# Two attention layers on one core: the values' products taken for four key blocks at a time, nine buffers of exponentials, new order tables

## The reference

```python
# layer 0, per image
h = group_norm(x, 32 groups) * gn_w + gn_b
q, k, v = split(qkv_w @ h + qkv_b)              # per head: 32 x 1024 each
w = softmax((q * s).T @ (k * s))                # 1024 x 1024, 8 heads
y = x + proj_w @ (v @ w.T) + proj_b
# layer 1, per image
q, k, v = Wq @ y, Wk @ y, Wv @ y                # 32, 32, 256 rows
out = gamma * (v @ softmax(q.T @ k).T) + y
```

## Time and profile before

| | |
|---|---|
| median of three runs | 1522.86 us |
| profiled execution, its own time | 1526.38 us |
| its span, first to last instruction | 1524.6 us |
| TensorE, matmuls: busy | 1483.1 us, 97% |
| GpSimd busy | 1185.9 us, 78% |
| VectorE busy | 1099.2 us, 72% |
| ScalarE busy | 746.4 us, 49% |
| mean granted TensorE clock | 0.977 of full |

### The profile page before, as it was taken

One profiled execution on the slowest core, in us unless ns is written; L12 is line 12 of the kernel. 1 busy time (PEld: TensorE's weight loads), 2 busy tenths in 40 slices (PEclk: granted clock), 3 DMA queues, 4 the chain that ended last, 5 costly groups with the idle time before them and its releaser, 6 DMA issues.

```text
span 1524.6 us, 20547 instructions
## 1 busy us (share of the span) xinstructions
PE 1483.1 (97%) x7216; PEld 891.4 (58%) x7216; DVE 1099.2 (72%) x1922; ACT 746.4 (49%) x1373; POOL 1185.9 (78%) x548
## 2 busy tenths in 40 slices
PE   8899999999999999999999999999999999999878
PEld 6444445577455855558555775558555684457447
DVE  4777878777787778877687777877788686765343
ACT  2256455544565354653555445653546435554411
POOL 2189988985989679995989859896799959898703
PEclk9699899999999999999999999999999999999979
DMA  5233031301403014120413014030231214000100
GB/s 140 55 96 68 17 87 46 83 10 49 112 22 84 15 56 102 39 65 28 112 50 79 12 51 111 22 84 15 60 100 41 60 31 109 22 1 8 49 21 28
DMA packets 47143, 85.24 MB, mean 56 GB/s; under 512 B 11072, under 2 KB 21184, under 8 KB 47040
## 3 DMA queue, kind: packets, MB, share of 16 engines
q1 hardware_dynamic: 46896, 83.74, 21.7%
q10 hardware_dynamic: 144, 0.20, 0.1%
HBM read 18.29 MB, written 8.39 MB: 17 GB/s over the span
## 4 chain that ended last, share of the span: by engine, by line
PE 87%; DVE 5%; SPq 3%; issue 2%; ACT 1%; DMA 1%; POOL 0%; ACTq 0%; DVEq 0%; POOLq 0%
PE work L635 15%; PE st L551 15%; PE pv L582 15%; PE pv L560 14%; PE work L698 7%; PE work L669 4%; DVE mpart L931 3%; PE work L705 3%; PE work L657 3%; SPq L386 3%; PE st L543 2%; PE work L643 2%; PE rec L599 2%; PE work L663 1%; PE rec L612 1%
## 5 line engine op out<-in xcount | busy, mean ns | idle before, releaser
L902 POOL TENSOR_TENSOR acc<-acc,probs 128x1024 f32<-128x1024 f32 x380 | 889.7, 2382 | 49.1 <-ACT probs L773 49.1
L773 ACT ACTIVATE probs<-st 128x512 f32<-128x512 f32 x1152 | 611.2, 601 | 446.1 <-PE st L551 326.7
L931 DVE TENSOR_REDUCE mpart<-work 128x1 f32<-128x512 f32 x1008 | 635.8, 680 | 164.8 <-PE work L635 163.2
L635 PE MATMUL work<-ks,qs 96*128 96x512 f32 x1008 | 427.0, 464 | 8.7 <-DMA ks<-part_hi 3.6
L551 PE MATMUL st<-qs,ks 98*128 98x512 f32 x1024 | 398.3, 436 | 6.2 <-DMA qs<-mrow 3.1
L902 POOL TENSOR_TENSOR acc<-probs 128x1024 f32<-128x1024 f32 x64 | 150.9, 2376 | 165.6 <-ACT probs L773 165.3
L635 PEld LDWEIGHTS work<-ks,qs 96*128 96x128 f32 x1008 | 191.7, 193 | 148.9 <-DVE mpart L931 87.9
L551 PEld LDWEIGHTS st<-qs,ks 98*128 98x128 f32 x1024 | 193.7, 191 | 126.1 <-ACT probs L773 67.8
L560 PE MATMUL pv<-probs,vt 128*32 128x512 f32 x2048 | 247.9, 602 | 0.0
L582 PE MATMUL pv<-probs,l_vt 128*128 128x256 f32 x1024 | 240.2, 383 | 0.5 <-ACT raw L839 0.5
L582 PEld LDWEIGHTS pv<-probs,l_vt 128*128 128x128 f32 x1024 | 193.2, 191 | 34.1 <-ACT probs L773 5.9
(11 more groups left out here) (82 smaller groups left out, 940.0 us busy)
## 6 DMA issues: line engine op xcount, KB each, us to landing
qs<-part_hi SPq DMA_DIRECT2D x120, 128.0 KB, 2.4
ks<-part_hi SPq DMA_DIRECT2D x120, 128.0 KB, 2.4
xa<-in_x SPq DMA_DIRECT2D x16, 512.0 KB, 4.3
y<-in_x SPq DMA_DIRECT2D x8, 1024.0 KB, 5.6
out<-raw SPq DMA_DIRECT2D x32, 256.0 KB, 2.2
qs<-part_lo SPq DMA_DIRECT2D x60, 128.0 KB, 2.4
ks<-part_lo SPq DMA_DIRECT2D x60, 128.0 KB, 2.4
l_qs<-part_hi SPq DMA_DIRECT2D x32, 64.0 KB, 2.0
```

The source lines that it names most:

```text
L635: last = mm(bank, qs[g][0:HI_HI_LO, c, j, tb * P:(tb + 1) * P], ks[g][0:HI_HI_LO, j, half * HALF:(half + 1) * HALF], start=True, stop=True)
L773: nc.scalar.activation(probs[:, n % PRING, half * HALF:(half + 1) * HALF], st[:, (2 * n + half) % ST_BANKS, :], ACT.Exp).then_inc(s_exp1 i ...
L902: pool.tensor_tensor(a, first, probs[:, n % PRING, :], ALU.add).then_inc(s_add0, 1)
L931: last = dve.reduce_max(mpart[:, 4 * j + tb, half:half + 1], bank, AX.X)
```

## The change

- `PRING` is 9 instead of 6. The memory comes from `raw1`, which is no longer a tile of its own: layer 1's results now lie in `xa`, and the low parts of `QF` in `y`. `mrow` is shared by the two groups of heads.
- Bursts stand at n % 8 == 1 and take four key blocks: 16 matmuls in the program, 32 in the trace. There are 64.
- The load of the next image into `xa` waits until the stores of the step before are done; the first load of `y` stands behind the stacking of `qs` and `ks` of the second group; `T` waits for the other group's rows.
- ScalarE, at slots with n % 8 == 1, serves the entries of the first two stops ahead of its exponentials.
- All four tables have new numbers. In the epilogue layer 1's first token half (`QK1`, `VT1` for n = 0) now stands ahead of the last `SUM`, and one `VT1` stands behind all maxima and their transposition.

```diff
-PRING = 6
+PRING = 9
...
 EPILOGUE = {
-    "sums": (2, 3, 3, 3, 3),
-    "layer1": (0, 0, 5, 6, 7, 9, 9, 10, 12, 13),
-    "maxima1": (11, 11, 11, 11, 15, 15, 15, 15, 15, 15, 15, 15, 15, 15, 15, 15, 16, 17),
+    "sums": (2, 10, 11, 11, 11),
+    "layer1": (0, 0, 0, 1, 6, 11, 11, 11, 17, 53),
+    "maxima1": (23, 33, 33, 33, 33, 33, 33, 33, 33, 33, 33, 33, 33, 33, 33, 33, 42, 42),
...
-        raw1 = sb("raw1", [P, 4, KT, QUARTER])
...
-        mrow = [[sb(f"mrow{g}{c}", [16, 2, P], F32R) for c in range(2)] for g in range(GROUPS)]
+        mrow = [sb(f"mrow0{c}", [16, 2, P], F32R) for c in range(2)]
...
+        def raw1(c):
+
+            return xa[:, c // 2, c % 2 * HALF:(c % 2 + 1) * HALF].rearrange("p (m t) -> p m t", m=KT)
...
                     sp.wait_ge(s_h, KT * (b + 1))
+                    if b > 0:
+                        for c in range(4):
+                            sp.wait_ge(s_out[c], 16 * b)
                     for k in range(KT):
                         sp.dma_start(xa[:, k, :], x_v[b + 1, :, k, :]).then_inc(s_x, 16)
...
                     if n == 1 and kind not in ("prologue", "first"):
-                        product_l0(SLOTS - 3, b - 1)
-                        product_l0(SLOTS - 1, b - 1)
-                    elif n % 4 == 1 and n - 5 in units and unit_use(n - 2)[0] == 0:
+                        for m in range(SLOTS - 7, SLOTS, 2):
+                            product_l0(m, b - 1)
+                    elif n % 8 == 1 and n - 9 in units and unit_use(n - 2)[0] == 0:
                         ci = unit_use(n - 2)[1] // 16
-                        if unit_use(n - 2)[1] % 16 == 3:
+                        if unit_use(n - 2)[1] % 16 == 7:
...
-                        product_l0(n - 4, b)
-                        product_l0(n - 2, b)
+                        for m in range(n - 8, n, 2):
+                            product_l0(m, b)
...
-                    entries = [e for k in range(STOPS) for e in plans[kind][STOPS * n + k]]
+                    stops = [plans[kind][STOPS * n + k] for k in range(STOPS)]
+                    before = stops[0] + stops[1] if n % 8 == 1 else []
+                    for e in before:
+                        use_entry(e, kind, b)
                     if n in units:
                         exponentials(n, kind, b)
```

More of the change, by code:

```diff
@@ L61 @@
+    "qk1": (193, 196, 196, 203),
+    "norm": (27, 34, 35, 42, 52, 70, 84, 100, 109, 110, 120),
+    "sums": (10, 14, 14, 16, 23, 72, 74, 75, 100, 118, 134, 135, 135, 141, 146, 153, 154, 154, 154, 157),
+    "sums1": (159, 159, 159, 162, 164, 164, 170, 171, 175, 175, 193, 193),
+    "v0": (181, 206),
+    "layer1": (4, 7, 32, 33, 38, 55, 88, 112, 139),
+    "v1": (14, 16),
+    "maxima": places(1, 0, 1, 2, 2, 2, 1, 0, 0, 1, 2, 2, 0, 0, 0, 3, 1, 1, 1, 1, 0, 0, 1, 0, 2, 0, 1, 0, 0, 0, 1,
[6 rows of a table added]
 }
 FIRST = {
-    "qf": (7, 7, 8, 8),
@@ L77 @@
+    "qk1": (158, 193, 208, 209),
+    "norm": (31, 31, 31, 42, 48, 53, 55, 104, 105, 107, 110),
+    "sums": (60, 72, 85, 87, 109, 118, 122, 151, 156, 158, 177, 179, 192, 203, 206),
+    "v0": (193, 212),
+    "v1": (32, 48),
+    "maxima": places(4, 0, 1, 0, 0, 1, 1, 0, 0, 0, 0, 3, 0, 2, 0, 0, 0, 0, 0, 0, 0, 0, 0, 2, 0, 0, 0, 2, 0, 1, 0,
[6 rows of a table added]
 }
 LAST = {
[L79 to L80 removed]
@@ L938, in use_bank @@
                         ahead = 1 if (g, c) == (0, 0) else 0
-                        rows, src, done, hi_done, n = (mrow[g][c], bank[0:16, 0:P], s_mrow[g][c], s_mhi[g][c], b + ahead)
-                        if kind not in ("prologue", "first") or (kind == "first" and ahead):
-                            dve.wait_ge(done, 32 * n)
+                        rows, src, hi_done, n = mrow[c], bank[0:16, 0:P], s_mhi[g][c], b + ahead
+                        if g:
+                            dve.wait_ge(s_mrow[0][c], 32 * (b + 1))
+                        elif n > 0:
+                            dve.wait_ge(s_mrow[1][c], 32 * n)
                     else:
```

70 lines of the change are left out of this document (30 added, 40 removed), and 36 rows, old and new, of tables (EPILOGUE, FIRST, LAST, STEADY).

## The result

The changed kernel takes 1516.56 us in the median of five runs (1513.55 to 1517.52), against 1522.86 (1521.46 to 1525.66, five runs) of the kernel before beside it: a ratio of 0.9947, with the interval 0.9936 to 0.9959, so 8.1 us less (the two medians themselves are 6.3 apart). Forecast were 23.3 less. The time lies at the upper edge of the range.

The account below looks back on a forecast made before the run. TensorE, busy 97%, was taken as the bound, with GpSimd 10.6 us behind in the long stretch. Terms -23.9 + 7 - 2 - 4.4 = -23.3 us gave a forecast of 1499.5 us, range 1485 to 1517.

Parts of the forecast that it names:

- (1): TensorE's bursts of products: 128 become 64, 63 of them count at 0.38 us each, 23.9 us less.
- (2): Waits behind longer bursts, with VectorE idle 1.8 us in each: 1.0 us a step, +7 in all, at worst +17.
- rival A: VectorE's idle time in each burst is paid by TensorE afterwards: 1511.6 us, chance 0.17.
- (3): Nine buffers of exponentials: needed for the long bursts, but little gain by themselves, 0 us.
- (4): Moved tiles, later loads, shared `mrow` and ScalarE's new order: 0 us; up to 1 us a step if the load's cover goes.
- (5): First step: less TensorE work before slot 10 brings first units and everything after earlier, -2 us, ends -6 and +3.
- (6): The end, from the last `SUM` to layer 1's scores: moved work fills idle time, -4.4 us, ends -7 and +1.
- D: The 0.4 us belong to each pair of key blocks, so merging bursts saves nothing: 1516 us, chance 0.07.
- C: GpSimd runs dry in bursts and sets a slower pace: 1525 us at 1 us a step, 1548 at 5; chance 0.08.

Follow-up runs that it names:

- both readers are light: Layer 0's maxima over half the keys and most exponentials over half the queries, in both kernels: 1488.17 us on the kernel before, 1462.89 on the changed kernel.
- the light GpSimd: GpSimd's additions from the second of a chunk on over half the elements, in both kernels: 1521.61 us on the kernel before, 1514.04 on the changed one.
- the new end alone: The kernel before with only the epilogue's new table: 1519.4 us, 0.996 of the kernel before.
- VectorE light: Layer 0's maxima reduced over 256 of 512 keys, in both kernels: 1497.16 us on the kernel before, 1486.57 on the changed kernel.

## Why the prediction was wrong

**(1) The bursts: right in price.** 0.375 us each against 0.38, from starts in one steady step, and 18.1 us for 48 bursts where both readers are light.

**(2) The waits behind a longer burst: right in kind, too small, and with only half of the cause.** I had 1.0 us a step; it is (18.0 - 9.4) / 6 = 1.4. I named VectorE, and ScalarE "likewise" had three exponentials, but I priced only VectorE's 89%. Measured, neither is the payer alone: either reader of the banks takes back about half of the bursts' price even when the other is light (a maximum 0.42 us instead of 0.68, an exponential 0.38 instead of 0.60). The Trainium skill, "TensorEngine Tiling (Array Packing)", section Performance Considerations, which I weighed under rival A, warns that tiling leaves the emptying of PSUM as it is; the trace agrees in that the two emptying engines together hold back half of the gain. Both kernels are tiled alike, so what tiling itself does to the emptying no run here shows.

**(3) Nine buffers, (4) the moved tiles: right for the steady steps**, 1066.6 against 1067.6 us. Not for the first step with its old table, where the missing slots 48 to 55 make slot 56 wait for the unit before it: 2.8 us and more, gone with ten buffers. In the changed kernel the tenth buffer brings nothing there.

**(5) The first step: the step that failed.** Predicted -3.7 with its seven bursts and the wait, measured +4.7: 8.4 of the 12.6 us by which the profiles miss the forecast. Its ground was that GpSimd works 79.5 of 80 us there, "so what brings the first units earlier moves everything after". The first units do come earlier, 1.5 us at slot 10, but nothing after moves with them: at slot 18 the step is 2.6 us behind, at its end 4.7. And the light GpSimd has 64 us less to do in the step and ends it no sooner (199.9 against 199.3). A full engine was taken for the bound. Instead, table and bursts each cost time by themselves. With the old table the long bursts add 3.4 to 4.2 us (205.3 against 202.0 and 201.1) though they save seven ways in and out; with short bursts the new table is 1.6 to 3.3 us dearer than the old one (203.6 and 204.4 against 202.0 and 201.1), the smaller figure within the scatter of 2.4. Together they are no dearer than either alone. Which wait of TensorE carries this stays open.

**(6) The end: right between its marks, and in part by luck.** From `SUM` to the scores it is 4.4 us less, as forecast. But the sum took what moved ahead of `SUM` for free. There the changed kernel is 2.0 us longer, though most of the last step's eight bursts (3.0 us) are saved in it; with the new end alone it is 4.0 longer. What was not in the sum, 3.6 us less from the scores to the end, where the granted clock is 0.97 instead of 0.89, makes up for most of that: -6.0 for the last step and the end instead of -7.4.

**The sum** was to be -23.3. By the stages it is +4.7 - 9.4 - 6.0 = -10.7, by the ratio of the runs -8.1. Rival A had 1511.6 us, "(2) is +17 or more, and (5) gives nothing": nearer in size than the forecast, but its mechanism, VectorE alone, is only half of what happens. (D's 1516 us lies nearest of all, by accident: its mechanism, a cost that is not the burst's, is excluded by the starts.) GpSimd as the bound, C, is excluded by the light GpSimd. The signs that I had named for the forecast mostly came: 3.57 us a burst, some 176 us from `P` to `P`, 31.7 us from `SUM` to the scores, no doubled wait of weight loads for VectorE. Only VectorE's own wait for the maxima fell where it was to grow. None of them looked at the first step or at the time ahead of `SUM`, so they could not tell that the sum would fail.

## What to carry to other kernels

Merging short runs of another shape saved a fixed price each time, here 0.375 us, and stretched the gap in which the other readers get nothing. Whether the saving stayed depended on both engines that empty TensorE's banks: lightened one at a time, the test said "not this one" for each of them. So lighten the suspects together as well before you let one go. Ask of work that is moved what it pushes back where it goes, and name a sign for each stage of the sum. A row of waits that appears (92.8 us) or a full engine (79.5 of 80 us) is a suspicion, and one more buffer or a halved operation settles it for a few runs.

## What the runs showed of the hardware

The order at the end bears on the clock of the last 40 us: with 3.27 us of idle time ahead of the scores the first sixteen products took 5.86 us and the stretch had a granted clock of 0.89; with `VT1` in that gap they took 3.62 us, at 0.97 to 1.00, in eleven of 13 profiles, and 4.8 us, at 0.92, in two.

The way into narrow matmuls cost 0.10 to 0.20 us in the bursts shown and the way out 0.13, whether 16 or 32 of them stood between. The Trainium skill, "TensorEngine Tiling (Array Packing)", section Tiling Modes, says that a change of the mode drains the engine; these rows show its price here. Not all of the way in is that: in the earlier trace rows the burst's first weights had waited for ScalarE's exponentials, as the timeline of the weight loads shows, and with VectorE light the mean way in is 0.12 us instead of 0.16.

```profile
786.69 0.16 PEld L560 LDWEIGHTS pv<-probs,vt 128*32 128x32 f32 x8 [0.24 <-ACT probs L773]
```

In the first step a single burst of 32 can fall into a spell of the lower level; on the timeline of after it is 5.27 us instead of 3.64:

```profile
83.77 5.27 PE L567 MATMUL pv<-probs,vt 128*32 128x512 f32 x32
```

and the window of it has a granted clock of 0.65:

```profile
83.77:88.50 4.73, 4.73 (x33) 1.15 (x32) 3.10 (x6) 1.08 (x2) 3.09 (x2) 0.65 0.31 126
```

Over the whole first step the mean is 0.93 before and after, so such spells don't explain its length. They do move time within it: up to slot 18 the mean is 0.84 before and 0.81 after, behind slot 18 0.97 and 0.98.

```profile
55.58:105.80 50.22, 49.05 (x199) 26.35 (x199) 35.94 (x79) 23.90 (x44) 30.40 (x13) 0.84 0.40 106
...
53.51:106.33 52.82, 50.86 (x200) 28.20 (x199) 36.62 (x79) 25.11 (x44) 32.82 (x14) 0.81 0.33 81
```
